# Factor bounds in the bank of P5 for quads with adapter groups, factors first in VectorE's loop, and 14 instead of 18 adapter groups in the first superblock

## What is computed

```
scale = cond @ norm_w.T + 1.0
h = x * (scale[:, None, :] * jax.lax.rsqrt(ms + EPS))
u = h @ up_w.T
val, gate = jnp.split(u, 2, axis=-1)
h = val * jax.nn.gelu(gate, approximate=False)
y = hq @ wq.T + x                       # hq, wq: quantised h and down_w
dWd = ((h_lang @ Wdd.T + bdd) * DELTA_SCALE).reshape(B, BN, D)
dWu = ((h_lang @ Wdu.T + bdu) * DELTA_SCALE).reshape(B, D, BN)
down = relu(y @ (Wd + dWd).T + bd);  out = y + down @ (Wu + dWu).T + bu
```

## Time and profile before

| | us |
|---|---|
| median of 3 runs | 865.9 |
| lowest, highest | 865.81, 866.25 |
| the profiled execution | 866.98 |
| its span, first to last instruction | 865.2 |
| TensorE busy in the span | 846.8 (98%) |
| superblock 0's quads 1 to 15 | from 42.9 to about 213 |

### The profile page before, as it was taken

How to read it: one execution, slowest core, us unless ns; L and a number is a source line. 1 busy time by engine, 2 the same in 40 slices (tenths; PEclk the granted TensorE clock), 3 DMA queues, 4 the chain that set the end, 5 groups by cost and what they waited for, 6 DMA issues and landing times.

```text
span 865.2 us, 11930 instructions
## 1 busy us (share of the span) xinstructions
PE 846.8 (98%) x4026; PEld 373.9 (43%) x4026; DVE 608.4 (70%) x942; ACT 389.9 (45%) x632; POOL 73.9 (9%) x79
## 2 busy tenths in 40 slices
PE   6999999999999999999999999999999999999998
PEld 5334444444444444444444444444444444444443
DVE  5997666888897765547886664658986764445986
ACT  5678776767545542216545543216433332214000
POOL 0453223210200000000200000000200000000100
PEclk9999999999999999999999999999999999999999
DMA  9879988659788876556587674634447443432231
GB/s 347 308 242 306 332 282 306 219 174 325 246 297 303 312 252 219 204 192 206 207 309 240 230 277 144 203 108 137 144 133 223 137 160 119 159 104 85 98 122 73
DMA packets 64283, 183.50 MB, mean 212 GB/s; under 512 B 7008, under 2 KB 8032, under 8 KB 64224
## 3 DMA queue, kind: packets, MB, share of 16 engines
q1 hardware_dynamic: 63936, 182.48, 60.5%
q10 hardware_dynamic: 288, 0.26, 0.1%
HBM read 152.31 MB, written 29.36 MB: 210 GB/s over the span
## 4 chain that ended last, share of the span: by engine, by line
PE 90%; ACT 3%; DVE 3%; DMA 2%; issue 2%; SPq 0%; POOL 0%; ACTq 0%; DVEq 0%; POOLq 0%
PE aux_ps L1114 10%; PE b_ps L1025 9%; PE b_ps L1029 9%; PE b_ps L1027 9%; PE a_ps L1025 6%; PE a_ps L1027 6%; PE a_ps L1029 6%; PE aux_ps L1070 6%; PE aux_ps L1177 3%; PE aux_ps L1168 3%; PE c_ps L1029 3%; PE c_ps L1027 3%; PE c_ps L1025 3%; PE e_ps L1027 3%; PE e_ps L1029 3%; PE e_ps L1025 3%
## 5 line engine op out<-in xcount | busy, mean ns | idle before, releaser
L1513 DVE SCALAR_TENSOR_TENSOR h_ring<-v_sb,unscale,gelu 128x512 f32<-128x512 f32 x63 | 48.4, 768 | 97.7 <-ACT gelu L836 54.8
L812 ACT ACTIVATE b_ps<-a_ps 128x512 f32<-128x512 f32 x63 | 36.7, 582 | 152.7 <-PE a_ps L1029 152.7
L1025 PE MATMUL b_ps<-t_mov,u_l 128*128 128x512 f16 x252 | 95.5, 379 | 1.6 <-DVE c_ps L1474 1.6
L1029 PE MATMUL b_ps<-t_mov,u_l 128*128 128x512 f16 x252 | 95.5, 379 | 0.0
L1027 PE MATMUL b_ps<-t_mov,u_l 128*128 128x512 f16 x252 | 95.5, 379 | 0.0
L1537 DVE TENSOR_TENSOR hmax<-gelu,hmax 128x512 f32<-128x512 f32 x120 | 82.4, 687 | 6.6 <-ACT gelu L842 1.0
L1114 PE MATMUL aux_ps<-h_ring,wq 128*128 128x512 f16 x384 | 84.9, 379 | 0.3
L711 POOL PARTITION_ALL_REDUCE yscale<-hmax x8 | 17.9, 2266 | 603.0 <-DVE hmax L1537 602.3
L842 ACT ACTIVATE gelu<-h_ring 128x512 f32<-128x512 f32 x64 | 40.3, 630 | 53.0 <-DVE h_ring L1523 52.0
L846 ACT ACTIVATE gelu<-h_ring 128x512 f32<-128x512 f32 x64 | 40.3, 630 | 51.1 <-DVE h_ring L1513 51.1
L1523 DVE SCALAR_TENSOR_TENSOR h_ring<-b_ps,unscale,gelu 128x512 f32<-128x512 f32 x64 | 47.9, 749 | 21.7 <-PE b_ps L1029 21.6
(11 more groups left out here) (217 smaller groups left out, 1640.8 us busy)
## 6 DMA issues: line engine op xcount, KB each, us to landing
w_ring<-in_Wdu SPq DMA_DIRECT2D x64, 512.0 KB, 6.2
w_ring<-in_Wdd SPq DMA_DIRECT2D x56, 512.0 KB, 6.9
u_l<-ul_dram SPq DMA_DIRECT2D x48, 512.0 KB, 4.5
u_e<-ue_dram SPq DMA_DIRECT2D x48, 384.0 KB, 3.1
h_ring<-in_up_w SPq DMA_DIRECT2D x16, 512.0 KB, 7.1
x_sb<-in_x SPq DMA_DIRECT2D x8, 1024.0 KB, 8.1
res<-in_down_w SPq DMA_DIRECT2D x16, 512.0 KB, 6.3
ul_dram<-u_l SPq DMA_DIRECT2D x15, 512.0 KB, 7.6
```

Of the source, the lines that this page charges most:

```text
L1025: pe.matmul(ps[:, :], weight(n, p, 0, k), hi, start=fresh and k == 0, stop=False, skip_group_check=True)
L1029: mm = pe.matmul(ps[:, :], weight(n, p, 1, k), hi, start=False, stop=k == 1, skip_group_check=True)
L1513: dve.scalar_tensor_tensor(out=h_slot(n)[:, TB:TS], in0=val[:, :], scalar=unscale[:, s // 2, j:j + 1], in1=gelu2[:, :], op0=ALU.mult, op1= ...
```

## The change

1. `DW_QUADS` moves its second corner from 26 to 22 groups. Superblock 0 now has 14 groups, after quads 3, 5, 7, 9, 11, 13 and 15, never after two quads in a row. The other 42 come after quads 17 to 42.
2. In the quads 1 to 13 that have groups, `bounds(n)` writes into `e_ps` instead of a bank of `aux_ps`, with a semaphore of its own. Before it TensorE waits for `keep_p5(n)`, and P5(n+1) waits until VectorE has read it.
3. `u_scale` and `power` stand first in VectorE's iteration, ahead of parts 2 and 3 of `u_low`.
4. Around quads 1 and 2: ScalarE does `keep_p5(1)` before `u_high(2, 0)` and `row_sums(4)`; VectorE does `u_low(3, 0)` after `seed_c(2)`.

```diff
-DW_QUADS = ((1, EARLY), (NP, 26), (43, NG))
+DW_QUADS = ((1, EARLY), (NP, 22), (43, NG))
+def bound_behind_groups(n):
+    return 1 <= n < NP - 2 and len(groups_of_quad(n)) > 0
...
-    if n + 2 < NP:
+    if n + 2 < NP and not bound_behind_groups(n):
         work.append(("bounds", n))
...
+        def bounds_read(n):
+            return (s_top, n + 4) if n + 3 < NP else (s_umul, 3 * (n + 2) + 3)
...
 # ScalarE
                 seed_b(n)
-                if n == 1:
-                    u_high(2, 0)
-                    row_sums(4)
...
                 keep_p5(n)
+                if n == 1:
+                    u_high(2, 0)
+                    row_sums(4)
...
 # TensorE, product P5
                         pe.wait_ge(s_p5sb, n - 1)
+                    if bound_behind_groups(n - 1):
+                        pe.wait_ge(*bounds_read(n - 1))
                     ps = e_ps
...
             def bounds(n):
-                ps = take("bounds", n)
+                if bound_behind_groups(n):
+                    pe.wait_ge(s_p5sb, n)
+                    ps = e_ps
+                else:
+                    ps = take("bounds", n)
...
-                mm.then_inc(s_aux, 1)
+                mm.then_inc(s_bounds if bound_behind_groups(n) else s_aux, 1)
...
 # VectorE
             for n in range(1, NQ):
+                if s == 0 and 1 < j and j + 1 < NP:
+                    u_scale(j + 1)
+                if s == 0 and 1 < j and j + 2 < NP:
+                    power(j + 2)
                 if s == 0 and j > 1:
                     u_low(j, 2)
                     u_low(j, 3)
...
                 if s == 0:
-                    if 1 < j and j + 1 < NP:
-                        u_scale(j + 1, bank("bounds", j - 1)[:, P:P + 1])
-                    if 1 < j and j + 2 < NP:
-                        power(j + 2)
-                    if 1 < j and j + 1 < NP:
+                    if 2 < j and j + 1 < NP:
                         u_low(j + 1, 0)
...
                     seed_c(n)
+                    if n == 2:
+                        u_low(3, 0)
```

More of the change, by code:

```diff
@@ L377, in build @@
         s_us = sem("s_us")
+        s_bounds = sem("s_bounds")
         s_first_hi = sem("s_first_hi")
@@ L417, in aux_ready, with bounds_ready @@
             eng.wait_ge(s_aux, aux[key] + 1)
+        def bounds_read(n):
+            return (s_top, n + 4) if n + 3 < NP else (s_umul, 3 * (n + 2) + 3)
+        def bounds_ready(eng, n):
+            if bound_behind_groups(n):
+                eng.wait_ge(s_bounds, sum(bound_behind_groups(q) for q in range(n + 1)))
+                return e_ps
+            aux_ready(eng, "bounds", n)
+            return bank("bounds", n)
         def bank_free(key):
@@ L426, in bank_free @@
                 "turn": (s_top, 1),
-                "bounds": (s_top, i + 4) if i + 3 < NP else (s_umul, 3 * (i + 2) + 3),
+                "bounds": bounds_read(i),
                 "mean": (s_mean, 1),
@@ L1229, in _ @@
                     product(n, 7)
-                for key in side_work(n):
-                    if key[0] == "dw":
-                        adapter_group(key[1])
-                    elif key[0] == "stat":
+                for g in groups_of_quad(n):
+                    adapter_group(g)
+                if bound_behind_groups(n):
+                    bounds(n)
+                for key in side_work(n)[len(groups_of_quad(n)):]:
+                    if key[0] == "stat":
                         stat(key[1])
@@ L1290, in power @@
             def power(j):
-                key, count = (("turn", 0), 3) if j == 0 else (("bounds", j - 3), 1)
-                aux_ready(dve, *key)
+                if j == 0:
+                    aux_ready(dve, "turn", 0)
+                    ps, count = bank("turn", 0), 3
+                else:
+                    ps, count = bounds_ready(dve, j - 3), 1
                 top, bits = um_top[0:1, 0:count], um_top[0:1, 0:count].bitcast(I32)
-                row = bank(*key)[0:1, 0:P * count].rearrange("p (n m) -> p n m", n=count)
+                row = ps[0:1, 0:P * count].rearrange("p (n m) -> p n m", n=count)
                 if j == 1:
@@ L1312, in u_unscale, with u_scale @@
                                       cs_pow[:, b:b + 1], ALU.mult, ALU.mult).then_inc(s_umul, 1)
-            def u_scale(j, pow_):
-                aux_ready(dve, "bounds", j - 2)
+            def u_scale(j):
+                pow_ = bounds_ready(dve, j - 2)[:, P:P + 1]
                 u_multiplier(j, pow_)
@@ L1663, in _ @@
             moving_sum(0, T1)
-            u_scale(1, bank("bounds", -1)[:, P:P + 1])
+            u_scale(1)
             power(2)
@@ L1676, in _ @@
             u_low(1, 3)
-            u_scale(2, bank("bounds", 0)[:, P:P + 1])
+            u_scale(2)
             power(3)
```

## The result

The changed kernel takes 876.8 us (median of four runs, 874.16 to 877.11) beside 866.1 us for the kernel before. The ratio is 1.0114, with a 95% interval from 1.0091 to 1.0136: slower by 10.7 us. I had forecast 869.7 us, with a range up to 873.0. The direction was right, the size was not.

What follows compares the result with a forecast made beforehand. TensorE, busy 846.8 of 865.2 us, was taken as the bound, so only its gaps count. Terms -4.1 + 0.2 + 4.6 + 3.1 = +3.8 us on a median of 865.9 gave 869.7 us, range 864.0 to 873.0.

Steps and rivals of the forecast that it cites:

- The gain, 4.1 us expected: Waits removed in quads 1 to 14: 3.3 us bank, 0.2 us spread roots, 0.4 and 0.2 us seed_c in quads 2 and 1.
- 3.3 us for the bank: Five waits of the bounds' transpose (L1138) for ScalarE's copy of a group; all 3.3 us go with the bounds in e_ps.
- The handshake, 0.2 us: P5(n+1) waits for VectorE on its bank: 0 to 0.25 us in each of six quads, 0.2 us in all, 1.5 at most.
- Quads 5 and 11, 2.3 us each: Tiles held behind load_d after an empty quad make the bounds late: 1.6 to 2.9 us each, 4.6 us in all.
- quads 7 and 9 stay as they are: Both already followed an empty quad whose load_d waits, so the new placement adds no loss there.
- Quad 3, 3.1 us: Tiles issued behind the block of x land late: a loss of 1.7 to 4.5 us, the middle taken.
- Quads 13 and 15 are safe: In both quads the tiles would not be late, as no load_d follows iteration 10; no loss counted.
- Quads 16 on should show no new gaps: Four groups moved into that stretch cost TensorE the same 0.96 us each, so this term is zero.
- rival 1: Tiles of quads 3, 5 and 11 come in time and the gain stands: -3.9 us, 862.0 us; chance 0.15.
- (2): Tiles late, but at the terms' lower ends: about +0.8 to +1.5 us, 866.7 to 867.4 us; chance 0.13.
- (3): P5 also waits for VectorE in six quads, 0.25 us or more each: 871.0 us or more; chance 0.08.
- rival 4: Statistic, spread roots and mean in quads 9, 11 and 13 still wait for an aux_ps bank: 0.2 us each; no chance given.

Runs made afterwards that it cites:

- bank_alone: The changed kernel with the old placement of the groups (18 in superblock 0): 864.3 us, ratio 0.9971 to the kernel before.
- early_18: tiles_early with the old placement of the groups (18 in superblock 0): 860.3 us, ratio 0.9928 to the kernel before.
- before_early: The kernel before, with only the tiles of quads behind an empty one issued an iteration earlier in superblock 0: 864.2 us, ratio 0.9964.
- old_later_aux: old_later with the bounds behind the groups back in aux_ps: 866.6 us, ratio 0.9994 to the kernel before.
- tiles_early: The changed kernel with, in superblock 0, tiles of a quad behind an empty one issued at the top of SyncE's iteration before: 861.8 us, ratio 0.9950.
- ahead_of_load_d: The changed kernel with the tiles of quads 5, 7, 9 and 11 issued in the iteration before, just ahead of load_d: 869.4 us, ratio 1.0035.
- x_behind_tiles: The changed kernel with the four tiles of quad 3 issued just ahead of the block of x in iteration 2: 870.8 us, ratio 1.0042.
- old_later: tiles_early with groups from quad 17 on placed as in the kernel before, two extra pairs after quads 29 and 36: 859.6 us, ratio 0.9921.
- x_behind_22: tiles_early with the block of x of SyncE's iteration 21 issued behind the four tiles of quad 22: 865.0 us, ratio 0.9984 to the kernel before.
- late_factors: old_later with u_scale and power back behind parts 2 and 3 of u_low on VectorE: 867.8 us, ratio 1.0006 to the kernel before.

## Why the prediction was wrong

- **The gain, 4.1 us expected:** 3.4 us by the quads that have no late tiles. Its 3.3 us for the bank was right as a list of waits and wrong as a price. Where the tiles are late the removed wait shows next to nothing (quads 5, 7 and 9 of bank_alone; items 2 to 4 of the change bring 2.1 us in all). With the same 18 groups and the tiles in time, items 2 to 4 bring about 3 us (early_18 beside before_early, 486.4 and 489.4 us from quad 1 to quad 43). With the 14 groups of the new placement the bank alone is worth 7.0 us (old_later_aux), slow clock included. The 0.8 us in quad 2 are twice what I took, and come from the order of VectorE's loop, not from item 4 by itself.
- **The handshake, 0.2 us:** right for the changed kernel, where no wait of P5 shows. The reason "ahead of them are only `val2` and two `sums_low`" left out the roots in iteration 10 and the scaling of x; they cost 0.5 us in bank_alone.
- **Quads 5 and 11, 2.3 us each:** quad 11 loses 2.2 us against tiles_early, as expected, quad 5 1.4 us. That quads 7 and 9 stay as they are was right to 0.2 us. The mechanism (`load_d` held by ScalarE) is shown by ahead_of_load_d.
- **Quad 3, 3.1 us: the step that failed most.** It loses 7.9 us against tiles_early, 6.4 us with the usual start of quad 1, and x_behind_tiles gives 6.0 us back in the median. The order of the queue was seen, but its price was mis-sized: I took the middle between an x that costs nothing and one behind which the tiles must wait, and no row spoke for a middle. The tiles do wait for all of x, and x took 9.5 to 9.8 us where I gave it its own 7.6. I let the last tile land at 75.4 in the worst case; it landed at 75.9 to 76.6 in the four kernels that issue x first. The rest is that TensorE was there at 68.1 and not at 70.0, as quad 1 began 1.8 us early (69.5 in ahead_of_load_d), which the tiles' landing follows only in part. And I gave a long wait no price beyond its length; the half clock adds up to 0.9 us.
- **"Quads 13 and 15 are safe: there is no `load_d` after iteration 10":** right for quad 13, wrong for quad 15, 1.5 us. With `load_d` out of the way, `put_e(n+1)` pins the tiles. It goes out 9.5 us after the start of quad 14, and quad 14 without groups is 9.06 us long. SyncE issues the tiles at 205.35, in quad 15 itself, and the row of the last ones is:

```profile
215.58 1.05 PE L1088 MATMUL aux_ps<-w_ring,cond_sb 128*32 128x512 f32 x4 [0.15 <-DMA w_ring<-in_Wdd]
```

- **"Quads 16 on should show no new gaps":** wrong, 2.5 us. The cost of four more groups there is zero, as taken, but the pattern shifts. A pair of groups is also 2 us in which VectorE catches up (quad 35), and its transfers stand in a queue with x (quad 22). I had looked at the number of groups in that stretch and not at which quads lose theirs.

The forecast was 6.9 us short. In the table, quad 3 is 4.8 us of that (3.3 with the usual start of quad 1), quads 22 and 35 are 2.5 and quad 15 is 1.5; the gain was 0.7 us smaller, and quads 5 and 11 lost 1.3 us less than forecast.

The rivals: the tiles were not in time (rival 1), nor at the lower ends (2), nor did the handshake cost (3). The waits of rival 4 appear once the tiles are in time, at 0.5 and 0.6 us.

The Trainium skill (TensorE: Matmul & The Clock Gate, Part 1) gives about 427 ns from start to start for 512 columns at 1.2 GHz and 216 ns at 2.4 GHz. The trace agrees: in old_later_aux the matmuls of P5 of quad 6 follow each other at 0.43 us at half clock, elsewhere at 0.21 to 0.22 us. The Trainium skill's figure of about 358 GB/s as the HBM limit of a core (DMA: Bandwidth & Descriptors, Specifications) is passed here too: 424 GB/s from 72 to 74 us in the changed kernel, where the tiles land 1.23 to 1.26 us apart. The lower rate was not the reason for the loss.

## What to carry to other kernels

Work that is placed in slots carries two things with it, the transfers that feed it and the time it gives to the other engines. Before moving it, look for each new slot at what the issuing engine waits for between the last use and the next, and for each slot that is emptied at which engine had used its length to catch up. Here the early issue of the tiles, a few lines, turned a loss of 10.7 us into a gain: tiles_early takes 861.8 us, 0.5% less than the kernel before, and old_later, with the old pattern in the later quads, 859.6 us, 0.8% less. And a wait seen in a profile is a price only with everything else in time: the listed 3.3 us brought 2.1 us with late tiles, together with the new orders, and the bank alone 7.0 us in the new placement with the tiles in time.

## What was not expected of the hardware

- A wait can cost about twice its length. After 4.1 us idle the granted clock was 0.50 while the groups of quad 3 ran. After waits of 1.2, 1.7 and 1.8 us directly behind groups (ahead_of_load_d and x_behind_22 in quad 22, old_later_aux in quad 5) it was at half for some 3.5 us of the next quad, at a cost of 1.7 us each. The length alone does not decide. In old_later_aux a wait of 1.03 us behind the groups of quad 9 was followed by the half clock, and one of 1.12 us at the same place of quad 11 was not, nor was one of 1.13 us in the profiled execution of the kernel before. It also differs between executions of one kernel: three of the eight runs of tiles_early have a mean clock of 0.998 and take 863.5 to 864.9 us, the other five 0.999 or 1.0 and 860.8 to 861.9 us. And in late_factors TensorE waited 2.5 us ahead of P5 in quad 12, behind P1 and not behind groups, and the clock stayed. The windows of that place:

```profile
166.00:168.00 2.00, 0.79 (x4) 0.42 (x5) 1.00 (x7) 0.00 (x0) 0.00 (x0) 1.00 1.09 354
168.00:170.00 2.00, 2.00 (x11) 0.88 (x9) 0.27 (x1) 0.99 (x2) 0.00 (x0) 1.00 0.90 329
```

- The order of a 1 MB block and four tiles of 512 KB in one queue changed the time for all of them: 11.9 us from first issue to last landing with the tiles in front (60.7 to 72.6), 15.4 us with the block in front (60.4 to 75.9), at 235 to 328 GB/s in the middle; in the three other kernels with the block in front it was 14.5 to 14.9 us. Part of it can be read from what follows. Behind the tiles, four more transfers of 384 or 512 KB land at 77.1, 78.4, 79.6 and 80.6, as far apart as the tiles did, while hardly anything moves any more:

```profile
78.00:80.00 2.00, 2.00 (x11) 1.05 (x11) 1.56 (x8) 0.70 (x2) 0.00 (x0) 1.00 0.08 31
```

  So most of their bytes had moved before, ahead of the last bytes of the tiles, and what landed late was a last share of each. That fits a few of the 16 DMA engines falling behind the others while x moved, with every landing waiting for the slowest; which engines, and why, no row shows, so the cause stays open.
